# Last layer's experts: scattered output rows, and the splitting of down weights and activations on other engines

## The reference

```
x_flat = x.reshape(T, D)                      # T = 2048 tokens, D = 256
shared = silu(x_flat @ shared_w1.T) @ shared_w2.T
gate_logits = x_flat @ gate_w.T               # 8 experts
top_k_gates, top_k_idx = top_k(gate_logits, 2)
top_k_gates = softmax(top_k_gates)
h = einsum('td,ehd->teh', x_flat, experts_w1)             # hidden width 1024
expert_out = einsum('teh,edh->ted', silu(h), experts_w2)
selected = sum over e of expert_out[t, e] * gates[t, e]
x = layernorm(x + shared + selected)
```

## Time and profile before

| | us |
|---|---|
| median of 3 runs | 3388.6 |
| lowest, highest | 3382.0, 3391.19 |
| span of the profiled execution | 3419.0 |
| TensorE busy | 3115.7 (91%) |
| VectorE busy | 1875.7 (55%) |
| ScalarE busy | 1705.1 (50%) |
| GpSimd busy | 1520.5 (44%) |
| the last expert part in the span | about 2979 to 3419 |

### The profile page before, as it was taken

The page is one execution under the profiler, slowest core; times in us unless marked ns, Lnnn a source line. Parts: engine busy times, 40 slices in busy tenths (PEclk is TensorE's granted clock), DMA queues, the critical chain, the costliest instruction groups (busy, mean ns, idle before and its releaser), DMA issues. The chain is left out here.

```text
span 3419.0 us, 59989 instructions
## 1 busy us (share of the span) xinstructions
PE 3115.7 (91%) x23982; PEld 2628.8 (77%) x23993; DVE 1875.7 (55%) x3913; ACT 1705.1 (50%) x3695; POOL 1520.5 (44%) x1146
## 2 busy tenths in 40 slices
PE   6997999999698898998997989799997999889995
PEld 5776888888575565897665868678886888789995
DVE  4764222223566465776554754467775666565554
ACT  4763332332276554554654653356665666535553
POOL 0222344434212675674234651233334454539984
PEclk9998999999799999999998999899999999999998
DMA  1002000100000010442001010110001000036652
GB/s 65 3 11 79 19 19 19 38 1 1 23 3 23 1 50 1 149 168 75 3 3 43 8 50 1 39 50 1 1 1 38 6 6 1 26 115 217 223 181 74
DMA packets 49794, 156.96 MB, mean 46 GB/s; under 512 B 9322, under 2 KB 29438, under 8 KB 37104
## 3 DMA queue, kind: packets, MB, share of 16 engines
q1 hardware_dynamic: 45776, 142.90, 12.2%
q0 software_dynamic: 3744, 10.23, 1.0%
HBM read 142.06 MB, written 10.26 MB: 45 GB/s over the span
## 5 line engine op out<-in xcount | busy, mean ns | idle before, releaser
L1303 POOL TENSOR_TENSOR prob<-prob,inv 128x512 f32<-128x512 f32 x320 | 331.6, 1042 | 401.3 <-DVE inv L1355 391.8
L1193 ACT ACTIVATE prob<-banks,nmax 128x256 f32<-128x256 f32 x640 | 297.3, 474 | 155.1 <-DVE nmax L1349 155.0
L2682 POOL TENSOR_TENSOR hL<-product,hH 128x512 fp32r<-128x512 f32 x128 | 165.9, 1296 | 321.5 <-ACT hH L2629 321.5
L2288 DVE TENSOR_REDUCE nmax<-banks 128x4 f32<-128x1024 f32 (+1 forms) x192 | 217.5, 1133 | 153.7 <-PE banks L1870 85.9
L2727 DVE TENSOR_TENSOR product<-banks,silu 128x512 f32<-128x512 f32 x128 | 88.6, 692 | 388.6 <-PE banks L2553 333.4
L2621 ACT ACTIVATE silu<-banks 128x512 f32<-128x512 f32 x128 | 76.5, 598 | 367.6 <-PE banks L2553 367.6
L1349 DVE TENSOR_REDUCE nmax<-banks 128x2 f32<-128x512 f32 x320 | 215.4, 685 | 20.6 <-PE banks L1172 16.2
L2553 PE MATMUL banks<-xH,upH 128*128 128x512 f32 x512 | 202.1, 395 | 5.8 <-POOL upL L2669 5.8
L2553 PE MATMUL banks<-xL,upH 128*128 128x512 f32 x512 | 201.5, 394 | 0.0
L2553 PE MATMUL banks<-xH,upL 128*128 128x512 f32 x512 | 199.9, 390 | 0.0
L3364 ACT ACTIVATE banks<-banks 128x512 f32<-128x512 f32 x124 | 71.9, 584 | 213.9 <-PE banks L3308 186.8
(11 more groups left out here) (617 smaller groups left out, 11026.6 us busy)
## 6 DMA issues: line engine op xcount, KB each, us to landing
W<-in_L_ffn_experts SPq DMA_DIRECT2D x80, 1024.0 KB, 5.4
W<-in_L_ffn_experts SPq DMA_DIRECT2D x8, 1536.0 KB, 7.9
slots_y<-W SPq DMA_DIRECT2D x23, 256.0 KB, 6.1
W<-strips SPq DMA_DIRECT2D x4, 768.0 KB, 7.5
W<-in_L_ffn_experts SPq DMA_DIRECT2D x9, 256.0 KB, 4.9
X<-in_x SPq DMA_DIRECT2D x1, 2048.0 KB, 8.3
cs<-in_ctxT SPq DMA_DIRECT2D x16, 128.0 KB, 2.3
W<-in_L_ffn_experts SPq DMA_DIRECT2D x1, 2048.0 KB, 7.6
```

The costliest lines, as they stand in the source:

```text
L1193: ins = nc.scalar.activation(m_.prob[p % 2][:, e * 512 + j * S:e * 512 + (j + 1) * S], bank(key)[:, j * S:(j + 1) * S], ACT.Exp, bias=m_.n ...
L1303: nc.gpsimd.tensor_tensor(pr, pr, m_.inv[:, slot(p, e):slot(p, e) + 2].unsqueeze(2).to_broadcast([P, 2, S]), ALU.mult)\
L2288: nc.vector.tensor_reduce(m_.nmax[b % 2][:, 2 * parts * i_:2 * parts * (i_ + 1)].rearrange("p (e q) -> p e q", e=2), scores.rearrange("p e ...
L2682: nc.gpsimd.tensor_tensor(m_.hL[:, at], m_.product[s % 2][:, :], m_.hH[:, at].bitcast(F32), ALU.subtract).then_inc(g.h_low.sem, 1)
```

## The change

Five things change, all in the last part.

1. The y rows of a block are no longer stored in slot order by SyncE. GpSimd scatters them, a tile of 128 rows at a time, to `rows_y`, where the row is the token's number plus 2048 for a second choice. A new column table `place` holds the rows; its building changes `mark_tiles` and `find_tokens`, and ScalarE's part of that table goes to VectorE. The chosen rows of a batch are then read by SyncE with two plain transfers of 256 KB (`load_choices`), and the 32 gathers go.
2. The down weights' low part is subtracted by VectorE, in four pieces of 128x512, two ahead of hL of quarter 0 and two ahead of hL of quarter 2. GpSimd keeps the up weights' low part, now in four pieces.
3. The down weights' high part is rounded by ScalarE at a unit's head, not at its end.
4. The activations are rounded by ScalarE in every unit, not by VectorE.
5. The end: batches are completed one unit earlier (0 in unit 27, then two a unit), and the last unit computes its y in two passes, one for each 128 tokens, with a normalization of its own for each (`end_tile`).

```diff
--- before.py
+++ after.py
@@ class Sparse @@
-        self.yg = [raw[i // 16][:, D * (i % 16):D * (i % 16 + 1)] for i in range(2 * NT)]
+        self.yg = [raw[b // 4][:, 4 * D * (b % 4):4 * D * (b % 4 + 1)] for b in range(B)]
...
+        self.place = sb("slot_places", TILES, U32)
+        self.offset, self.choice = sb("row_offsets", 2 * NT, F32), sb("choice_tiles", 2 * NT, F32)
@@ experts_sparse @@
-        return range(2 * (l - 1), 2 * l) if 1 <= l < B - FRONT else range(0)
+        return range(max(2 * l - 1, 0), 2 * l + 1) if 0 <= l < B - FRONT else range(0)
+
+    def next_weights(q):
+
+        w = weights_of(q)
+        return w + 1 if last_unit(w) == q and w + 1 < SETS else None
+
+    quarters = [slice(at, at + 512) for at in range(0, 2048, 512)]
...
@@ SyncE @@
-            def store_block(j):
-                freed(sp, ("y", FRONT + j))
-                sp.dma_start(slots_y[j * S:(j + 1) * S, :].rearrange("(t p) d -> p t d", p=P), m_.yb[j % 2].rearrange("p (t d) -> p t d", d=D))\
-                    .then_inc(g.block_stored[j % 2].sem, 16)
+            def load_choices(b):
+
+                filled(sp, ("u", FRONT + SLOTS + b // 4, b % 4))
+                for k in range(2):
+                    sp.dma_start(m_.yg[b][:, 2 * k * D:2 * (k + 1) * D].rearrange("p (t d) -> p t d", d=D),
+                                 rows_y[k * T + b * S:k * T + (b + 1) * S, :].rearrange("(t p) d -> p t d", p=P)).then_inc(g.gathered[b].sem, 16)
...
             for w in range(1, SETS):
                 load_weights(w)
-                if w >= 4:
-                    store_block(w - 4)
-            for j in range(SETS - 4, SLOTS):
-                store_block(j)
+
+            split(sp, g.up_low, SETS - 1)
+            split(sp, g.down_low, SETS - 1)
+            for parity in range(2):
+                sig = g.block_stored[parity]
+                sp.wait_ge(sig.sem, sig.base + 32 * ((SLOTS + 1 - parity) // 2))
+            for b in range(B):
+                load_choices(b)
...
@@ TensorE @@
+                if q == NQ - 1:
+                    for t, key in enumerate((("y", q), "last")):
+                        to = claim(key)
+                        for f in range(8):
+                            if t == 0 and f % 2 == 0:
+                                freed(pe, ("u", q, f // 2))
...
+                        done(key, mm)
+                    continue
@@ ScalarE @@
             for q in range(NQ):
 
-                after = weights_of(q) + 1 if last_unit(weights_of(q)) == q and weights_of(q) + 1 < SETS else None
+                after = next_weights(q)
+                if after is not None:
+                    down_high(after)
                 hidden(q, 0)
                 hidden(q, 1)
-                if q == 2:
-                    act.wait_ge(g.places_ready.sem, g.places_ready.base + 1)
-                    nc.scalar.activation(m_.tile_row.rearrange("p (i c) -> p i c", c=2 * TILES)[:, :, 0:TILES],
-                                         m_.at_tile.rearrange("p (i c) -> p i c", c=TILES), ACT.Copy, scale=m_.row).then_inc(g.places_ready.sem, 1)
                 if after is not None:
                     up_high(after)
-                if late(q) >= 0:
-                    hidden_high(q, 0)
+                hidden_high(q, 0)
                 hidden(q, 2)
-                if late(q) >= 0:
-                    hidden_high(q, 1)
+                hidden_high(q, 1)
                 hidden(q, 3)
-                if late(q) >= 0:
-                    hidden_high(q, 2)
-                    hidden_high(q, 3)
+                hidden_high(q, 2)
+                hidden_high(q, 3)
...
-                if after is not None:
-                    down_high(after)
@@ GpSimd @@
             def low(w):
                 split(pool, g.up_high, w)
-                nc.gpsimd.tensor_tensor(m_.upL[w % 2][:, :], raw[w % 2][:, 0:2048], m_.upH[w % 2][:, :].bitcast(F32), ALU.subtract)\
-                    .then_inc(g.up_low.sem, 1)
-                split(pool, g.down_high, w)
-                nc.gpsimd.tensor_tensor(m_.downL[w % 2][:, :], raw[w % 2][:, 2048:4096], m_.downH[w % 2][:, :].bitcast(F32), ALU.subtract)\
-                    .then_inc(g.down_low.sem, 1)
+                for at in quarters:
+                    ins = nc.gpsimd.tensor_tensor(m_.upL[w % 2][:, at], raw[w % 2][:, at], m_.upH[w % 2][:, at].bitcast(F32), ALU.subtract)
+                ins.then_inc(g.up_low.sem, 1)
+
+            def scatter(j, t):
+
+                if t == 0:
+                    freed(pool, ("y", FRONT + j))
+                    if j:
+                        sig = g.block_stored[(j - 1) % 2]
+                        pool.wait_ge(sig.sem, sig.base + 32 * ((j + 1) // 2))
+                else:
+                    sig = g.block_stored[j % 2]
+                    pool.wait_ge(sig.sem, sig.base + 32 * (j // 2) + 16)
+                i = 2 * j + t
+                nc.gpsimd.indirect_dma_start(rows_y, bass.IndirectOffsetOnAxis(ap=m_.place[:, i:i + 1], axis=0),
+                                             m_.yb[j % 2][:, t * D:(t + 1) * D], None).then_inc(g.block_stored[j % 2].sem, 16)
...
             for w in range(1, SETS):
                 low(w)
+                if w >= 3:
+                    scatter(w - 3, 1)
                 if w + 1 < SLOTS:
                     fetch(w + 1)
...
-            for t in range(NT):
-                for k in range(2):
-                    nc.gpsimd.indirect_dma_start(m_.yg[2 * t + k], None, slots_y,
-                                                 bass.IndirectOffsetOnAxis(ap=m_.slots[:, k * NT + t:k * NT + t + 1], axis=0))\
-                        .then_inc(g.gathered[t // 2].sem, 16)
-                if t in (9, 11):
-                    power(t // 2 - 4)
...
+                if w >= 2:
+                    scatter(w - 2, 0)
+            scatter(SLOTS - 1, 1)
...
@@ VectorE @@
-                for k in range(2):
-                    half = slice(k * NT, (k + 1) * NT)
-                    nc.vector.tensor_tensor(each(m_.tile_row, 2 * TILES)[:, half, TILES:2 * TILES], each(m_.at_tile, TILES)[:, half, :],
-                                            m_.count[:, 0:NT].unsqueeze(2).to_broadcast([P, NT, TILES]), ALU.mult)
+                nc.vector.tensor_scalar(m_.offset[:, :], m_.low, m_.row, None, ALU.subtract)
+                step(nc.vector.tensor_scalar(m_.choice[:, :], m_.count[:, 0:2 * NT], float(2 * NT), None, ALU.subtract))
+                for part, factor in enumerate((m_.offset, m_.choice)):
+                    ins = nc.vector.tensor_tensor(each(m_.tile_row, 2 * TILES)[:, :, part * TILES:(part + 1) * TILES], each(m_.at_tile, TILES),
+                                                  factor[:, :].unsqueeze(2).to_broadcast([P, 2 * NT, TILES]), ALU.mult)
+                ins.then_inc(g.places_ready.sem, 1)
...
+            def end_tile(t, key, n_):
+
+                filled(dve, key)
+                step(nc.vector.tensor_tensor(rows(t), bank(key)[:, 0:D], rows(t), ALU.add))
+                normalize_part1(nc, g, dve, lambda _: rows(t), 1, t, step, None)
+                dve.wait_ge(g.rstd_ready.sem, g.rstd_ready.base + n_ + 1)
+                normalize_part2(nc, g, lambda _: rows(t), 1, t, lambda _: g.X[:, t * D:(t + 1) * D]).then_inc(g.x_done.sem, 1)
...
                 for f2 in range(4):
                     key = ("u", q, f2)
                     at = slice(f2 * 512, (f2 + 1) * 512)
-                    if late(q) < 0:
-                        dve.wait_ge(g.h_raw.sem, g.h_raw.base + 4 * q + f2 + 1)
-                        nc.vector.tensor_copy(m_.hH[:, at], bank(key)[:, :]).then_inc(g.h_high.sem, 1)
+                    if f2 % 2 == 0 and after is not None:
+                        split(dve, g.down_high, after)
+                        for c in (quarters[f2], quarters[f2 + 1]):
+                            ins = nc.vector.tensor_tensor(m_.downL[after % 2][:, c], raw[after % 2][:, 2048:4096][:, c],
+                                                          m_.downH[after % 2][:, c].bitcast(F32), ALU.subtract)
+                        if f2:
+                            ins.then_inc(g.down_low.sem, 1)
                     dve.wait_ge(g.h_high.sem, g.h_high.base + 4 * q + f2 + 1)
...
-            take_y(NQ - 1)
-            freed(dve, ("y", NQ - 1))
-            for b in range(2 * (B - FRONT - 1), B):
-                complete(b)
+            dve.wait_ge(g.gathered[B - 1].sem, g.gathered[B - 1].base + 32)
+            for t in (NT - 2, NT - 1):
+                step(add_choices(t, g.X[:, t * D:(t + 1) * D]))
+            end_tile(NT - 2, ("y", NQ - 1), B - 1)
+            end_tile(NT - 1, "last", B)
```

More of the change, by code:

```diff
@@ L3182, in experts_sparse @@
         u.add(("y", q), 4 + q % 2)
+    u.add("last", 4 + NQ % 2)
     def bank(key):
@@ L3601, in rows, with add_choices @@
                 return m_.R[:, t * D:(t + 1) * D]
[L3603 to L3608 removed]
+            def add_choices(t, onto):
+                r, yg = rows(t), m_.yg[t // 2]
```

(6 more changed lines are left out.)

51 lines of the change are left out of this document (24 added, 27 removed).

## The result

The changed kernel takes 3478.7 us (median of 4, 3473.8 to 3482.9) against 3386.8 us, a ratio of 1.0268 with an interval of 1.0253 to 1.0284. It is slower, as forecast, but by 92 us and not by the forecast's 48: the time lies above the range's 3450.

The account below looks back on a forecast made before the run. TensorE was taken to bound the routed units. 3388.6 us + 50.5 (routed units) - 0.8 (head) - 1.3 (tail) = 3437.0 us, range 3400 to 3450 us.

Parts of the forecast that it names:

- no queue forms: GpSimd, routed units: scatters' landing waits cause no queue, four up pieces standing between; a scatter priced like a 0.95 us gather.
- The bound and its place: Routed units 4 to 26 are bound by TensorE, so lateness costs its full length; only head and tail have slack.
- The first wait, 0.65 us: Each routed unit: ScalarE rounds activations after the up weights, so TensorE's down matmuls start 0.65 us late.
- The second wait, 1.53 us: Each routed unit: VectorE's down pieces three and four wait for GpSimd's, so hL of quarter three reaches TensorE 1.53 us late.
- They take turns: VectorE and GpSimd, each reading two SBUF operands, alternate; the second waits for one whole instruction; a unit is 14.1 us.
- Rival 5, the clock: Gaps in each routed unit lower TensorE's granted clock, 1.1 us a unit, 25 us: 3462 us; chance 0.07.
- The head: Units 0 to 3: small delays and savings on VectorE and ScalarE, together -0.8 us; unit 3's first hL 0.4 us late.
- The tail: After unit 29's y VectorE is the bound; its closing work takes 7.8 us instead of 9.2: -1.3 us.
- The stall: Unit 28, beside the gathers: 25.3 us taken as mostly belonging to the profiled execution, so removal gains little in the median.
- rival 2: The stall beside the gathers is real in every execution and goes with them, with both delays: 3411.7 us; chance 0.12.
- Rivals 1 and 3: Rival 1: engines don't block each other, 3402 us (0.17); rival 3: with the gathers' stall real too, 3376.6 us (0.08).
- Rival 4: Routed units: the roundings find room after all, only head and tail change: 3386.5 us; chance 0.05.

Follow-up runs that it names:

- experiment 3: Changed kernel with all four down-weight low pieces ahead of quarter 0's hL, and activation quarters 0 and 1 rounded ahead of the up weights: 3428.4 us, ratio 1.0032.
- experiment 1: Changed kernel with all four low pieces of the down weights ahead of hL of quarter 0 on VectorE: 3425.9 us, ratio 1.0038.
- experiment 5: Changed kernel with four down pieces ahead of first hL, quarters 0 and 1 rounded ahead of up weights, no scatter landing wait: 3385.8 us, ratio 0.9912.
- experiment 7: Changed kernel without landing wait, a scatter directly ahead of GpSimd's four up pieces: 3538.9 us; with a small power there instead: 3487.6 us.
- experiment 4: Changed kernel with spare rows for each block's unused slots, so no scatter waits for another's landing: 3446.2 us, ratio 1.0087.
- experiment 6: Changed kernel without landing wait, GpSimd's up low part in pieces of 256, 512, 512, 512 and 256 columns: 3471.5 us.

## Why the prediction was wrong

The forecast was +48.4 us, the ordinary times differ by 91.9. Two steps of the working failed and a third was priced at nothing: landings that "no queue forms" behind, turns that are always taken, and the granted clock.

- **The bound and its place.** Right. Routed units had no slack, and every microsecond of lateness came out in full: +82.7 of the 87.8 us found.
- **The first wait, 0.65 us.** Right. Removing it (the first units of experiment 3 against those of 1) takes a unit from 12.66 to 11.94 us, 0.72.
- **The second wait, 1.53 us.** Right where the engines take turns: a unit is 13.96 us, 14.1 by the forecast. It failed at the step "They take turns": the earlier trace rows show one turn of one pair, and I made a rule of it. In ten of 22 units VectorE lost all turns, and piece 3 took 3.9 to 5.1 us, not 1.1; that cost 2.0 us more each.
- **"The scatter of a tile waits for the tile before to land, with the four up pieces between, so no queue forms."** This is the step that failed first. It holds for a block's second scatter. The first scatter of the next block has only two fetches between, 3.2 us, against landings of 5.6 to 7.7 us beside 2 MB of weights in the changed kernel ("7.4 us" in experiment 5's expectation is the time to the next scatter's start; the landing is 6.6). In the changed kernel that puts the scatter directly ahead of the pieces in every second unit (a unit of 13.96 us is too short for it, the 17 us behind it long enough), and experiment 7 shows what that does. Without the wait the forecast comes true (experiment 4: 14.3 us a unit against 14.1; of the 9 us that its total is off, most is the head). I priced the issue of a scatter (1.0 us, right) and not its landing.
- **Rival 5, the clock.** I gave it 0.07 because the waits were short. A wait of 1.7 us did bring a second half from 3.15 to 4.63 us in every other unit (experiment 6), and one of 2.8 us in the changed kernel. There it costs some 17 us, in ten units, and not 25 in 23; the forecast's own sum had nothing for it.
- **The head.** I had unit 3's first hL 0.4 us late and the whole head at -0.8. It became 5.5 us longer (75.7 to 81.2), since in unit 3, too, GpSimd's pieces stand directly behind a gather. With the pieces apart (experiments 3 and 5) the head is 73.1 and 73.4 us. The rows of the changed kernel:

```profile
3039.73 0.95 POOL L3488 DMA_INDIRECT W<-rows_x,slot_tokens  x1 [0.32 <-issue]
3040.70 4.98 POOL L3465 TENSOR_TENSOR upL<-W,upH 128x512 fp32r<-128x512 f32 x4
...
3040.69 6.14 DVE L3688 TENSOR_TENSOR downL<-W,downH 128x512 fp32r<-128x512 f32 x2
...
3047.49 0.58 PE L3364 MATMUL bank<-downH,hH 128*128 128x256 f32 x1 [4.06 <-DVE hL L3693]
```

- **The tail.** -1.3 was -0.4, between 63.7 and 63.3 us.
- **The stall.** Leaving it out of the sum gave the right number for the first comparison, but by luck: the stall belongs to the gathers, and ordinary executions can have it. On the experiments' chips rival 2's condition held, and the changed kernel is slower there by 1.8%, not 2.7%.
- **Rivals 1 and 3** fell with the blocking: experiment 1 shows what a unit without it is, 12.66 us. **Rival 4** fell with the first wait, which is there in every unit.

## What to carry to other kernels

Before you put a wait on a landed transfer, write down the issue that it waits for, all that stands between the two on the queue, and what other transfers start in the same microsecond: the landing's time is the term, not the issue's (6.6 us here, not 1.0). Where VectorE reads two SBUF operands, put it where GpSimd is idle, by order alone; a price for turns taken from one pair of instructions isn't a bound. And before a stall is put down to a profiled execution, take the suspected work out once: 26 us hung on it here.

## What was not expected of the hardware

- A VectorE subtraction with two SBUF operands waited through up to four GpSimd instructions in a row (4.7 us for the piece in all 22 units of experiment 7 with the scatter ahead; 1.0 us in the 22 of experiment 4, asked for at the same 0.81 us into a piece).
- 32 indirect gathers of 128 rows each in the last units cost 26 us of ordinary time. ScalarE stood still for 24.8 us, TensorE for 15.2 us in gaps that no row explains, at a lower granted clock beside; plain transfers of the same size from the same engine cost none.
- A scatter of 128 KB issued 0.01 us ahead of 2 MB of plain transfers landed 6.6 us later; the range in one kernel was 2.4 to 7.9 us.
- TensorE's granted clock behind a wait of 1.7 us fell to 0.63 in one unit and stayed at 1.00 in the next, with the same waits in both.
